# A new mixer pass: two query buffers, sums scaled first, rows before weights on ScalarE, and unread products on TensorE

## Chip, cores and metric

The kernel runs on one core of a Trainium2 chip. The core has five engines that run side by side and wait for each other through semaphores: TensorE (PE in the rows; PEld is its weight load), VectorE (DVE), ScalarE (ACT), GpSimd (POOL) and SyncE (SP, which here issues transfers). The metric is the time of one execution on the device in microseconds (us), the median of several runs.

## What is computed

The reference is one layer of a graph network over 6250 nodes with 256 features and 106250 edges.

```
xn = layernorm(x)
graph = relu([xn, mean of edge_attr per source node, u] @ W1 + b1) @ W2 + b2
m = xn
for i in range(4):                       # the mixer, four passes
    h = layernorm(m) * ln1_g[i] + ln1_b[i]
    q = softmax(h @ Wq[i], within each of 8 heads)
    k = softmax(h @ Wk[i], over the 6250 nodes)
    v = h @ Wv[i]
    m = m + (q @ (k^T v, per head)) @ Wo[i] + bo[i]
    h = layernorm(m) * ln2_g[i] + ln2_b[i]
    m = m + gelu(h @ mW1[i] + mb1[i]) @ mW2[i] + mb2[i]      # 256 -> 1024 -> 256
y = x + graph + m
out = y + (one of 32 small networks for each node, chosen by argmax of layernorm(y) @ rw^T + rb)
```

## The kernel before

**Tiles.** The nodes are 50 tiles of 125 rows. They are worked on in 25 pairs, called groups `g` (`GROUPS` = 25, `LAST` = 24). The running sum `m` stays in on-chip memory as `res`. The weights of the 256 -> 1024 -> 256 part are each kept as a high and a low half (`w1`, `w2`, as are `h1` and `hidh`), and each product is made as three products of halves (`mm3`).

**Order of the work.** Every engine has its own program. `passes(step, drain)` runs a first round of `step(-1, g)`, then `drain(-1)`, and then for the passes l = 0 to 3 the steps t = -1 to 24, with `drain(l)` behind the first three. In step (l, t) group t goes through the wide part (`up`, `gelu`, `hidden_low`, `down`, in four parts c = 0 to 3), group t + 1 through the attention's end (`transpose_queries`, `copy_queries`, `attend`, `attention_residual`, a root on GpSimd, `attention_normalise`, `attention_transpose`, `attention_high`, `attention_low`), and group t - 1 through the keys and queries of pass l + 1. The order on each engine is written out by hand, and each engine works strictly through its own list.

**The drain and the mixer's matrix.** The sums over all nodes (`acc` and `esacc`) are complete only when the last group has gone through. `drain` ends with `context`: `acc` is divided by `esacc` (two `tensor_scalar`, semaphore `c_scaled`), transposed on TensorE, made into `gn`, multiplied by Wv (`raw_vo[:, 0]`), masked into `ct`, multiplied by Wo and added to the bias: this is `mmat` (semaphore `c_ready`). `attend(l, g)` multiplies the queries of a group by `mmat`.

**Queries.** The finished softmax `qn` of a group (`softmax_queries`, `exp_queries`, `finish_queries`) is stored in device memory by SP (`store_queries`), and loaded in the next pass into the one buffer `qin` (`load_queries`, 250 KB). TensorE transposes it (`transpose_queries`, semaphore `q_T`), ScalarE copies it to `qT`. The load of group g waits until group g - 1 was transposed. In `step`, SP issues the load of group t + 2; in `drain` it issues that of group 0, after the store of the last group but one.

**Weights.** In the drain SP loads W2 into `raw` (`load_down`), after `w1` was made of the former contents of `raw`. At t = -1 ScalarE casts it to `w2`'s high half (`down_high`) and VectorE makes the low half (`down_low`). The first `down` of the pass waits for that, the first `up` for `h1`.

**GpSimd.** It takes the two roots of each step (`r1`, `r2`: one over the standard deviation), and between these it issues scatters of edge rows to device memory (L720), up to 12 a step in passes 0 to 2, for the segment sums of pass 3. The rows come in pieces through `load_attr` into `staging`.

**Pass 3** has no keys and queries of a later pass. In their place it sums edge rows per node (`seg_turn`, six pieces a step), with work on all five engines.

Of the kernel before, what the change touches and what calls it, by code (L numbers as in the profile page):

```python
# [5 lines left out]
F32 = mybir.dt.float32  # L6
# [10 lines left out]
P = 125  # L17
TILES = 50
D = 256
KC = D // 128  # L20
PAIR = 2
GROUPS = TILES // PAIR
# [23 lines left out]
IDLE_SCATTER = 48  # L46
IDLE_SEGMENT = 1
EH = 64
YROW = D + 4
# [49 lines left out]
def build(nc, x, src, edge_attr, u, gW1, gb1, gW2, gb2, Wq, Wk, Wv, Wo, bo, ln1_g, ln1_b, mW1, mb1, mW2, mb2,  # L99
# [9 lines left out]
    with ctx:  # L109
        def sb(name, shape, dt=F32, where=None):  # L110
            return (where or ctx).enter_context(nc.sbuf_tensor(name, shape, dt))
# [114 lines left out]
        qT = sb("qT", [128, KC, GT], F32, layers)  # L226
        qin = sb("qin", [P, PAIR, D], F32, layers)
        hid = [sb(f"hid{i}", [128, 2, GT], F32, layers) for i in range(2)]
# [10 lines left out]
        count16 = sb("count16", [128, KINDS - 1 + BOTH], BF16, layers)  # L239
        row16 = sb("row16", [BOTH, KINDS], BF16, layers)  # L240

        pos_f = stage[:, 0, :, :].rearrange("p c r -> p (c r)")[:, 0:ECOL]
# [94 lines left out]

        q_in, q_out, q_T, q_copied, a_prod, a_res = sems("q_in q_out q_T q_copied a_prod a_res")
        a_ve, a_root, a_xh, a_xT, a_hi, a_lo = sems("a_ve a_root a_xh a_xT a_hi a_lo")
# [32 lines left out]
        ATTR, SCATTERED = [attr0, attr1], [scattered0, scattered1]  # L372
        N_IN = [n_in0, n_in1]

# [133 lines left out]
        def _(sp):  # L508
# [44 lines left out]
            def load_queries(l, g):  # L553
                n = nth(l, g)
                sp.wait_ge(q_T, n)
                sp.wait_ge(q_out, 16 * (n + 1))
                sp.dma_start(qin[:, :, :], pair(query_rows[l % 2], g)).then_inc(q_in, 16)

# [43 lines left out]
            def step(l, t):  # L602
                if 0 <= l and t + 2 < GROUPS:
                    load_queries(l, t + 2)
                if l == 0 and t == -1:
                    load_attr(0)
                    load_attr(1)
                if l >= 0 and t == -1:
                    attr_after(l - 1, GROUPS)
                if l < LAYERS - 1 and t >= 2:  # L610
                    store_queries(l + 1, t - 2)
                attr_after(l, t)
                if l >= 0 and t == -1:
                    if l < LAYERS - 1:
                        load_mixer(l + 1)
                    if l < LAYERS - 1:
                        load_up(l + 1)
                if l == LAYERS - 1:
                    load_segments(t)

            def drain(l):
                store_queries(l + 1, LAST - 1)
                load_queries(l + 1, 0)
                load_down(l + 1)
                store_queries(l + 1, LAST)
# [176 lines left out]
        def _(act):  # L802
# [122 lines left out]
            def step(l, t):  # L925
# [7 lines left out]
                if t == -1:  # L933
                    copy_queries(l, 1)
                    down_high(l)
                segs = seg_turns(t) if l == LAYERS - 1 else ()
# [25 lines left out]
                if t + 1 < GROUPS:  # L962
                    attention_high(l, t + 1)

            def drain(l):
# [122 lines left out]
        def _(dve):  # L1088
# [353 lines left out]

            def context(l):
# [5 lines left out]
                a.then_inc(c_scaled, 1)  # L1449
                dve.wait_ge(c_T, l + 1)  # L1450
                for k in range(KC):
# [140 lines left out]
            def drain(l):  # L1592
# [20 lines left out]
                key_sum(L, final + 1)  # L1613
                add_block(L, BLOCKS - 1)
                softmax_queries(L, LAST)
                context(L)
# [182 lines left out]
        def _(pe):  # L1799
# [36 lines left out]
            def transpose_queries(l, g):  # L1836
                n = nth(l, g)
                pe.wait_ge(q_in, 16 * (n + 1))
# [4 lines left out]
                transposes(chunks(PQT), qin, P).then_inc(q_T, 1)  # L1843

# [75 lines left out]
            def queries_of(l, g):  # L1920
                m = nth(l, g)
                if l:
                    pe.wait_ge(a_res, nth(l - 1, min(g + 2, LAST)) + 1)
                if m:
                    pe.wait_ge(s_sub, m)
                for j in range(PAIR):
                    for k in range(KC):
                        a = mm(PMQ[0:P, j * D:(j + 1) * D], h2[:, k, j * P:(j + 1) * P], wqk[:, k, D:2 * D], k == 0, k == KC - 1)
                a.then_inc(s_prod, 1)

            def max_transpose(l, b):
# [103 lines left out]
            def step(l, t):  # L2035
# [21 lines left out]
                if t == -1:  # L2057
                    transpose_queries(l, 1)
                for n in segs[2:3]:
                    seg_turn(n)  # L2060
# [24 lines left out]
                if attention:  # L2085
                    attention_transpose(l, t + 1)
                if later:
                    for g in WEIGH_AT.get(t, ()):
                        weigh(l + 1, g)
# [187 lines left out]
```

## Time and profile before

| | before |
|---|---|
| median of 3 runs | 3057.9 us (3054.7 to 3060.46) |
| the profiled execution | 3049.58 us |
| its span | 3047.8 us |
| mean granted TensorE clock | 0.947 |
| TensorE busy | 2687.7 us, 88% |
| VectorE busy | 2127.8 us, 70% |
| GpSimd busy | 1724.1 us, 57% |
| ScalarE busy | 1517.9 us, 50% |

The profile is of one execution. Its own time is 8.3 us under the median of the runs shown, so differences are worked out within it and then taken from the median. The busy share is a mean over stages: which engine sets the pace of a stage is read from the waits of that stage. In the rows "[2.23 <-DVE acc L1448]" says that the engine was idle for 2.23 us before the instruction and what ended that. The clock is a share of 2.4 GHz. The passes start (first product of `up`) at about 348, 888, 1441 and 1998 us.

### The profile page before, as it was taken

What the parts mean: (1) busy time and instruction counts of PE and PEld (TensorE: products, weight loads), DVE (VectorE), ACT (ScalarE), POOL (GpSimd) and SP (SyncE); (2) the same over time, 40 slices, a digit from 0 to 9 for tenths busy, and PEclk for the clock granted to TensorE, in tenths of its full rate; (3) what the DMA queues carried; (4) which work ended last, traced back from release to release, by engine and by line L of the source; (5) the groups of instructions that cost most, each with busy time, mean ns of one, the idle gap of its engine ahead of it and who ended that gap; (6) DMA issues with size and microseconds to landing.
All of it is one profiled execution on the core that took longest, in us unless ns stands there. A gap on an engine that the chain in (4) does not pass through costs nothing.

```text
span 3047.8 us, 56121 instructions
## 1 busy us (share of the span) xinstructions
PE 2687.7 (88%) x18842; PEld 2467.5 (81%) x18842; DVE 2127.8 (70%) x4836; ACT 1517.9 (50%) x2947; POOL 1724.1 (57%) x1611
## 2 busy tenths in 40 slices
PE   4888899999989999997999999978888888996298
PEld 2666799999978899996889999868888887996165
DVE  8887567776756667675566766678888886897054
ACT  0343366566535565663556666444444444773064
POOL 0011178777758888886788887045444554222666
PEclk8999899999979999997999999889999998998599
DMA  3000223322232232323232322043333332210343
GB/s 120 24 28 24 83 50 69 66 63 58 57 97 60 63 68 62 69 53 98 58 67 61 70 60 56 26 120 90 86 83 86 83 85 58 64 43 20 82 125 92
DMA packets 255489, 207.88 MB, mean 68 GB/s; under 512 B 165433, under 2 KB 194314, under 8 KB 255205
## 3 DMA queue, kind: packets, MB, share of 16 engines
q1 hardware_dynamic: 197606, 162.55, 19.9%
q0 software_dynamic: 57600, 41.75, 6.9%
q8 instruction: 155, 2.54, 0.4%
q14 instruction: 128, 1.05, 0.1%
HBM read 136.93 MB, written 70.16 MB: 68 GB/s over the span
## 4 chain that ended last, share of the span: by engine, by line
PE 20%; POOL 14%; issue 8%; DVE 7%; ACT 2%; DMA 1%; DVEq 1%; SPq 0%; ACTq 0%; POOLq 0%; another core or an unknown queue 0%
PE bank L376 18%; POOL edges_sorted L720 9%; POOL tokens_sorted L785 2%; DVE xh L1261 2%; PE bank L1803 1%; DVE hidh_lo L1297 1%; POOL r L698 1%; PE bank L2248 1%; DVE oh L1489 1%; POOL ehl L737 1%; DVE bn L1252 1%; ACT hidh_hi L832 1%; ACT ehl L908 1%; ACT hid L826 0%; DVE res L1269 0%
## 5 line engine op out<-in xcount | busy, mean ns | idle before, releaser
L720 POOL DMA_INDIRECT edges_sorted<-staging,pos_i x850 | 1061.6, 1249 | 252.2 <-issue 231.3
L826 ACT ACTIVATE hid<-bank,b1p 128x250 f32<-128x250 f32 x800 | 331.4, 466 | 400.0 <-PE bank L376 359.0
L376 PE MATMUL bank<-h_hi,w_hi 128*128 128x250 f32 x1600 | 483.1, 302 | 19.6 <-DVE h_lo L1281 19.5
L1297 DVE TENSOR_TENSOR hidh_lo<-hid,hidh_hi 128x500 fp32r<-128x500 f32 x400 | 296.6, 742 | 290.4 <-ACT hidh_hi L832 217.0
L376 PE MATMUL bank<-w_hi,hidh_hi 128*125 128x256 f32 x1600 | 467.8, 292 | 0.0
L376 PE MATMUL bank<-h_hi,w_lo 128*128 128x250 f32 x1600 | 451.8, 282 | 0.0
L376 PE MATMUL bank<-w_hi,hidh_lo 128*125 128x256 f32 x1600 | 451.1, 282 | 0.0
L376 PE MATMUL bank<-w_lo,hidh_hi 128*125 128x256 f32 x1600 | 450.0, 281 | 0.0
L376 PE MATMUL bank<-h_lo,w_hi 128*128 128x250 f32 x1600 | 448.4, 280 | 0.0
L376 PE MATMUL bank<-wqk,h 128*125 128x256 f32 x1600 | 377.5, 390 | 0.6 <-ACT mbc L877 0.6
L376 PEld LDWEIGHTS bank<-wqk,h 128*125 128x125 f32 x1600 | 304.0, 194 | 46.2 <-issue 1.2
L376 PEld LDWEIGHTS bank<-h_hi,w_hi 128*128 128x128 f32 x1600 | 307.5, 192 | 27.5 <-DVE h_lo L1281 24.1
L832 ACT CAST hidh_hi<-hid 128x500 fp32r<-128x500 f32 x400 | 243.7, 609 | 152.2 <-PE bank L376 115.2
L376 PEld LDWEIGHTS bank<-h_lo,w_hi 128*128 128x128 f32 x1600 | 308.9, 193 | 1.9
L376 PEld LDWEIGHTS bank<-h_hi,w_lo 128*128 128x128 f32 x1600 | 305.5, 191 | 0.0
L376 PEld LDWEIGHTS bank<-w_hi,hidh_hi 128*125 128x125 f32 x1600 | 298.8, 187 | 2.0
L376 PEld LDWEIGHTS bank<-w_lo,hidh_hi 128*125 128x125 f32 x1600 | 298.0, 186 | 2.1
L376 PEld LDWEIGHTS bank<-w_hi,hidh_lo 128*125 128x125 f32 x1600 | 297.4, 186 | 0.0
L698 POOL TENSOR_TENSOR r<-ve,minus_half 125x2 f32<-125x2 f32 x175 | 136.3, 779 | 280.9 <-DVE ve L1257 277.9
L1489 DVE TENSOR_TENSOR oh<-iota_node,kb 128x1000 fp32r<-128x1000 f32 x153 | 228.7, 1495 | 59.8 <-POOL kb L732 59.7
L1261 DVE TENSOR_SCALAR xh<-res,mv,r 125x256 f32<-125x256 f32 x350 | 160.1, 498 | 135.5 <-POOL r L698 135.5
L376 PE MATMUL bank<-ehl,oh 128*125 128x130 f32 x1224 | 164.3, 278 | 65.0 <-DVE agg L1477 65.0
(289 smaller groups left out, 5712.4 us busy)
## 6 DMA issues: line engine op xcount, KB each, us to landing
staging<-edges_sorted SPq DMA_DIRECT2D x103, 260.0 KB
staging<-in_edge_attr SPq DMA_DIRECT2D x50, 531.2 KB
queries<-qn SPq DMA_DIRECT2D x100, 250.0 KB
qin<-queries SPq DMA_DIRECT2D x100, 250.0 KB
edges_sorted<-staging,pos_i POOLq DMA_INDIRECT x850
rows_in<-edges_sorted SPq DMA_DIRECT2D x50, 260.0 KB
yin<-tokens_sorted SPq DMA_DIRECT2D x81, 127.0 KB
raw<-in_L_mix_W SPq DMA_DIRECT2D x8, 1024.0 KB, 6.6
```

What stands on the lines that cost most here:

```text
L376: return nc.tensor.matmul(o, left, right, start=start, stop=stop, skip_group_check=True)
L698: nc.gpsimd.tensor_tensor(o[:, :], ve[:, :], minus_half[:, :], ALU.pow).then_inc(done, 1)
L720: nc.gpsimd.indirect_dma_start(out=edges_sorted, out_offset=bass.IndirectOffsetOnAxis(ap=pos_i[:, i:i + 1], axis=0), in_=stage[:, slot, j, ...
L737: nc.gpsimd.tensor_tensor(ehl[n % 4][:, :, EA + 2:2 * EA + 2], rows_in[n % RIN][:, :, 0:EA], f32(ehl[n % 4][:, :, 0:EA]), ALU.subtract).th ...
L785: nc.gpsimd.indirect_dma_start(out=tokens_sorted, out_offset=bass.IndirectOffsetOnAxis(ap=fpos_i[:, t:t + 1], axis=0), in_=res[:, t, :], i ...
L826: a = nc.scalar.activation(hid[c % 2][:, j, :], chunks(PH[c % 2])[:, j, :], ACT.Gelu, bias=b1p[:, 2 * c + j:2 * c + j + 1])
L832: nc.scalar.copy(hidh[c % 2][0][:, :, :], hid[c % 2][:, :, :]).then_inc(f_hi, 1)
L908: nc.scalar.copy(ehl[n % 4][:, :, 0:EA], rows_in[n % RIN][:, :, 0:EA]).then_inc(s_hi, 1)
L1252: step_(nc.vector.bn_stats(st[:, j, :], res_row(PAIR * g + j)))
L1261: a = nc.vector.tensor_scalar(o[:, j, :], res_row(PAIR * g + j), mv[:, j, 0:1], r[:, j:j + 1], ALU.subtract, ALU.mult)
L1297: nc.vector.tensor_tensor(hidh[c % 2][1][:, :, :], hid[c % 2][:, :, :], f32(hidh[c % 2][0][:, :, :]), ALU.subtract).then_inc(f_lo, 1)
L1489: nc.vector.tensor_tensor(oh[n % 4][:, :, :], iota_node[:, :].unsqueeze(1).to_broadcast((128, SEGR, P)), kb[:, n % 4, :].unsqueeze(2).to_b ...
```

## The change

- There are two buffers `qin0`, `qin1` with a semaphore each. Group g + 2 may be loaded once group g was transposed. In `step` SP issues the load of group t + 3. In `drain` it issues those of groups 0 and 1, ahead of the last two stores.
- On VectorE the division of `acc` is a function of its own, `context_scale`, and runs ahead of `softmax_queries` of the last group.
- On ScalarE, at t = -1, `down_high` runs after `attention_high`, and a two-element Gelu (`warm_gelu`) between them.
- On TensorE, at t = -1, eight products of 128 columns whose result nobody reads follow the transposes of group 1's queries, and five more follow the transposes of group 0's `xh1`. They go to bank `PS`.

```
+IDLE_RESIDUAL, IDLE_HALVES = 8, 5
...
             def load_queries(l, g):
                 n = nth(l, g)
-                sp.wait_ge(q_T, n)
+                if n >= 2:
+                    sp.wait_ge(q_T, n - 1)
                 sp.wait_ge(q_out, 16 * (n + 1))
-                sp.dma_start(qin[:, :, :], pair(query_rows[l % 2], g)).then_inc(q_in, 16)
+                sp.dma_start(qin[n % 2][:, :, :], pair(query_rows[l % 2], g)).then_inc(Q_IN[n % 2], 16)
...
             def step(l, t):                                    # SP
-                if 0 <= l and t + 2 < GROUPS:
-                    load_queries(l, t + 2)
+                if 0 <= l and t + 3 < GROUPS:
+                    load_queries(l, t + 3)
...
             def drain(l):                                      # SP
+                load_queries(l + 1, 0)
+                load_queries(l + 1, 1)
                 store_queries(l + 1, LAST - 1)
-                load_queries(l + 1, 0)
                 load_down(l + 1)
                 store_queries(l + 1, LAST)
...
                 if t == -1:                                    # ScalarE, step
                     copy_queries(l, 1)
-                    down_high(l)
...
                 if t + 1 < GROUPS:
                     attention_high(l, t + 1)
+                if t == -1:
+                    warm_gelu()
+                    down_high(l)
...
-            def context(l):                                    # VectorE
+            def context_scale(l):
                 dve.wait_ge(g_acc, block(l, BLOCKS - 1) + 1)
                 step_(nc.vector.reciprocal(esrec[:, :], esacc[:, :]))
                 stepped()
                 for k in range(KC):
                     a = nc.vector.tensor_scalar(acc[:, k, :], acc[:, k, :], esrec[:, k:k + 1], None, ALU.mult)
                 a.then_inc(c_scaled, 1)
+
+            def context(l):
                 dve.wait_ge(c_T, l + 1)
...
                 add_block(L, BLOCKS - 1)                       # VectorE, drain
+                context_scale(L)
                 softmax_queries(L, LAST)
                 context(L)
...
             def transpose_queries(l, g):                       # TensorE
                 n = nth(l, g)
-                pe.wait_ge(q_in, 16 * (n + 1))
+                pe.wait_ge(Q_IN[n % 2], 16 * (n // 2 + 1))
...
-                transposes(chunks(PQT), qin, P).then_inc(q_T, 1)
+                transposes(chunks(PQT), qin[n % 2], P).then_inc(q_T, 1)
...
+            def idle_products(count):
+
+                for _ in range(count):
+                    mm(PS[:, 0:128], ident[:, :], ones[:, :], True, True)
...
                 if t == -1:                                    # TensorE, step
                     transpose_queries(l, 1)
+                    idle_products(IDLE_RESIDUAL)
...
                 if attention:
                     attention_transpose(l, t + 1)
+                if t == -1:
+                    idle_products(IDLE_HALVES)
```

## Rows read from the trace of the kernel before

**Rows 1.** Waits, whole run: engine, line waited for: us in total, times, longest.

```profile
PE bank L1803 <- DMA qin<-queries: 26.0, 5, 7.2
```

**Rows 2.** Timeline of TensorE, start of pass 1: start us, us, instructions.

```profile
865.65 0.66 PE L1982 MATMUL bank<-ident,acc 128*128 128x128 f32 x4 [2.23 <-DVE acc L1448]
...
867.39 2.08 PE L376 MATMUL bank<-gn,raw_vo 128*128 128x128 f32 x8
...
872.97 3.75 PE L376 MATMUL bank<-mmat,qT 128*125 128x256 f32 x8 [0.90 <-issue]
883.01 1.10 PE L1803 MATMUL bank<-ident,qin 125*128 125x125 f32 x4 [6.29 <-DMA qin<-queries]
883.90 1.04 PE L1803 MATMUL bank<-ident,xh 125*128 125x125 f32 x4
887.76 0.58 PE L376 MATMUL bank<-h_hi,w_hi 128*128 128x250 f32 x1 [2.82 <-DVE h_lo L1281]
```

**Rows 3.** Timeline of VectorE, end of the drain and start of pass 1.

```profile
861.93 0.87 DVE L1392 SCALAR_TENSOR_TENSOR acc<-acc,fexp_k,bank 128x256 f32<-128x256 f32 x2
863.45 0.69 DVE L1402 TENSOR_REDUCE qstat<-bank 125x16 f32<-125x512 f32 x1 [0.65 <-PE bank L376]
...
864.78 0.15 DVE L1445 RECIPROCAL esrec<-esacc 128x2 f32<-128x2 f32 x1
...
866.34 0.99 DVE L1452 TENSOR_SCALAR gn<-bank,cols 128x256 f32<-128x256 f32 x2 [0.75 <-PE bank L1982]
...
879.56 0.73 DVE L1261 TENSOR_SCALAR xh<-res,mv,r 125x256 f32<-125x256 f32 x2 [0.84 <-POOL r L698]
...
888.22 2.28 DVE L1440 TENSOR_TENSOR w_lo<-raw,w_hi 128x2048 fp32r<-128x2048 f32 x1
```

**Rows 4.** Timeline of ScalarE, start of pass 1.

```profile
884.62 1.90 ACT L896 CAST w_hi<-raw 128x2048 fp32r<-128x2048 f32 x1
886.41 0.58 ACT L846 CAST h_hi<-bank 128x500 fp32r<-128x500 f32 x1
890.75 1.28 ACT L826 ACT_TABLE_LOAD   x1 [3.76 <-issue]
```

**Rows 5.** Windows: us, each engine's busy us, granted clock, DMA share, GB/s.

```profile
866.00:873.00 7.00, 6.10 (x28) 5.10 (x26) 4.70 (x8) 1.10 (x2) 0.00 (x0) 0.54 0.04 8
873.00:877.00 4.00, 3.72 (x8) 2.45 (x8) 1.65 (x4) 0.00 (x0) 0.00 (x0) 0.52 0.83 290
877.00:880.00 3.00, 0.00 (x0) 0.00 (x0) 2.05 (x8) 0.00 (x0) 0.97 (x2) 1.00 0.31 78
...
888.00:894.00 6.00, 6.00 (x27) 5.81 (x28) 2.95 (x3) 3.21 (x6) 1.20 (x1) 0.51 0.91 257
894.00:897.00 3.00, 3.00 (x23) 2.83 (x22) 2.25 (x5) 1.05 (x3) 0.00 (x0) 1.00 0.81 302
```

**Rows 6.** Waits from 905 to 1412 us, the rest of pass 1.

```profile
DVE xh L1261 <- POOL r L698: 61.3, 29, 4.8
...
POOL r L698 <- DVE ve L1257: 0.5, 1, 0.5
```

**Rows 7.** Timeline of GpSimd, start of pass 1.

```profile
891.43 1.20 POOL L720 DMA_INDIRECT edges_sorted<-staging,pos_i  x1 [4.17 <-DMA staging<-in_edge_attr]
897.55 0.72 POOL L698 TENSOR_TENSOR r<-ve,minus_half 125x2 f32<-125x2 f32 x1 [4.92 <-DVE ve L1257]
```

**Rows 8.** Timelines of VectorE and TensorE, start of pass 3.

```profile
1989.41 5.88 DVE L1261 TENSOR_SCALAR xh<-res,mv,r 125x256 f32<-125x256 f32 x2 [0.80 <-POOL r L698]
...
1995.36 1.10 PE L1803 MATMUL bank<-ident,xh 125*128 125x125 f32 x4 [4.01 <-DVE xh L1261]
1997.83 0.58 PE L376 MATMUL bank<-h_hi,w_hi 128*128 128x250 f32 x1 [1.38 <-DVE h_lo L1281]
```

**Rows 9.** The chain in order of time, pass 3: start us, us, what.

```profile
2040.00 1.71 DVE xh L1261 x2
...
2062.29 1.71 DVE xh L1261 x2
```

More of the change, by code:

```diff
@@ L47 @@
 IDLE_SEGMENT = 1
+IDLE_RESIDUAL, IDLE_HALVES = 8, 5
 EH = 64
@@ L226, in build @@
         qT = sb("qT", [128, KC, GT], F32, layers)
-        qin = sb("qin", [P, PAIR, D], F32, layers)
+        qin0 = sb("qin0", [P, PAIR, D], F32, layers)
         hid = [sb(f"hid{i}", [128, 2, GT], F32, layers) for i in range(2)]
@@ L240, in build @@
         row16 = sb("row16", [BOTH, KINDS], BF16, layers)
+        qin1 = sb("qin1", [P, PAIR, D], F32, layers)
+        qin = [qin0, qin1]
         pos_f = stage[:, 0, :, :].rearrange("p c r -> p (c r)")[:, 0:ECOL]
@@ L335, in build @@
         w1_hi, w1_lo, w2_hi, w2_lo, b1_pe, b1_ready, b2_added = sems("w1_hi w1_lo w2_hi w2_lo b1_pe b1_ready b2_added")
-        q_in, q_out, q_T, q_copied, a_prod, a_res = sems("q_in q_out q_T q_copied a_prod a_res")
+        q_in0, q_in1, q_out, q_T, q_copied, a_prod, a_res = sems("q_in0 q_in1 q_out q_T q_copied a_prod a_res")
         a_ve, a_root, a_xh, a_xT, a_hi, a_lo = sems("a_ve a_root a_xh a_xT a_hi a_lo")
@@ L554, in load_queries @@
                 n = nth(l, g)
-                sp.wait_ge(q_T, n)
+                if n >= 2:
+                    sp.wait_ge(q_T, n - 1)
                 sp.wait_ge(q_out, 16 * (n + 1))
-                sp.dma_start(qin[:, :, :], pair(query_rows[l % 2], g)).then_inc(q_in, 16)
+                sp.dma_start(qin[n % 2][:, :, :], pair(query_rows[l % 2], g)).then_inc(Q_IN[n % 2], 16)
             def load_attr(c):
@@ L602, in step @@
             def step(l, t):
-                if 0 <= l and t + 2 < GROUPS:
-                    load_queries(l, t + 2)
+                if 0 <= l and t + 3 < GROUPS:
+                    load_queries(l, t + 3)
                 if l == 0 and t == -1:
@@ L621, in drain @@
             def drain(l):
+                load_queries(l + 1, 0)
+                load_queries(l + 1, 1)
                 store_queries(l + 1, LAST - 1)
-                load_queries(l + 1, 0)
                 load_down(l + 1)
@@ L934, in step @@
                     copy_queries(l, 1)
-                    down_high(l)
                 segs = seg_turns(t) if l == LAYERS - 1 else ()
@@ L963, in step @@
                     attention_high(l, t + 1)
+                if t == -1:
+                    warm_gelu()
+                    down_high(l)
             def drain(l):
@@ L1441, in down_low, with context_scale @@
                                         ALU.subtract).then_inc(w2_lo, 1)
-            def context(l):
+            def context_scale(l):
                 dve.wait_ge(g_acc, block(l, BLOCKS - 1) + 1)
@@ L1449, in context @@
                 a.then_inc(c_scaled, 1)
+            def context(l):
                 dve.wait_ge(c_T, l + 1)
@@ L1614, in drain @@
                 add_block(L, BLOCKS - 1)
+                context_scale(L)
                 softmax_queries(L, LAST)
@@ L1837, in transpose_queries @@
                 n = nth(l, g)
-                pe.wait_ge(q_in, 16 * (n + 1))
+                pe.wait_ge(Q_IN[n % 2], 16 * (n // 2 + 1))
                 if n:
@@ L1842, in transpose_queries @@
                 pe.wait_ge(g_acc, ALL_BLOCKS if l == LAYERS - 1 else block(l + 1, sum(s < g - 1 for s in SUM_AT)))
-                transposes(chunks(PQT), qin, P).then_inc(q_T, 1)
+                transposes(chunks(PQT), qin[n % 2], P).then_inc(q_T, 1)
             def attend(l, g):
@@ L1929, in queries_of, with idle_products @@
                 a.then_inc(s_prod, 1)
+            def idle_products(count):
+                for _ in range(count):
+                    mm(PS[:, 0:128], ident[:, :], ones[:, :], True, True)
             def max_transpose(l, b):
@@ L2058, in step @@
                     transpose_queries(l, 1)
+                    idle_products(IDLE_RESIDUAL)
                 for n in segs[2:3]:
@@ L2086, in step @@
                     attention_transpose(l, t + 1)
+                if t == -1:
+                    idle_products(IDLE_HALVES)
                 if later:
```

2 lines of the change are left out of this document (1 added, 1 removed).

## The prediction

> **What bounds the kernel now.** I read the waits first. One of them is special: five times TensorE waits for a transfer into `qin`, 26.0 us together, 7.2 us the longest [rows 1]. Four of these are the four mixer passes' starts, the fifth is 0.3 us. So I went on to the start of the second pass; the passes are numbered 0 to 3 here, and the other starts have the same form.
>
> The timeline of TensorE there reads as follows [rows 2]. The transposes of `acc` at 865.65 come after 2.23 us of standing still for VectorE. The mixer's matrix `mmat` is then built. At 872.97 the eight products of `attend` begin. The next thing in TensorE's order is the transpose of the second query pair, and it starts only at 883.01, when its transfer has landed. SP issues that transfer only behind the drain's last store. The transposes of `xh1` are behind it. The first product of `up` comes at 887.76. On VectorE `xh1` was finished at 879.56 + 0.73 = 880.29 [rows 3], so it stood ready for 3.6 us. On ScalarE the cast of all of `w2` (1.90 us from 884.62) runs ahead of the cast of `h1` at 886.41 [rows 4], although the transposes of `xh1` ended at 883.90 + 1.04 = 884.94 [rows 2]. TensorE is at half its clock (0.51 to 0.54, which is 1.2 GHz) from 866 to 873 and again from 888 to 894, and back at 1.00 only from 894 [rows 5].
>
> Does time won at a pass's start reach the end? It does if the engine that paces the pass is moved too. In the first pass that is TensorE. In the second it is GpSimd: VectorE waits 29 times for GpSimd's roots, 61.3 us, while GpSimd waits for VectorE's variances once, 0.5 us [rows 6]. Its scatters stand in one queue with those roots. So what counts in passes 1 and 2 is when GpSimd takes the second root of the pass (897.55, after an idle time of 4.92 us for VectorE) [rows 7].
>
> **The change, part by part.**
>
> *Sums scaled first* (`context_scale` ahead of `softmax_queries`). Now the last `acc` operation ends at 861.93 + 0.87 = 862.80. VectorE waits until 863.45 for the product of queries and does the softmax, and only then, from 864.78, scales `acc` [rows 3]. TensorE follows at 865.65 [rows 2] and `gn` at 866.34. Afterwards the scaling (865.65 - 864.78 = 0.87 us with its reciprocal and the signal) starts at 862.8 and is done about 863.7, the transposes run 863.7 to 864.4, and the softmax (1.33 us from start to start) runs beside them and ends near 865.0. So `gn` starts at 865.0 instead of 866.34: **1.3 us**, in four passes. What waits on the softmax is `exp_queries` on ScalarE, behind a copy of `qT` that comes much later; it costs nothing.
>
> *Two buffers and earlier loads.* In the drain both first loads are issued ahead of the last two stores. Both conditions (the row stored, the buffer's earlier pair transposed) were met some steps before, so SP's queue isn't held there, and both transfers (250 KB) have some 20 us. In `step` each load goes one pair further. Its wait on `q_T` is still for the same transpose as before, so what is queued behind it on SP (attributes, stores, mixer weights) is not held longer. The load of pair 2 takes the place of that of pair 1 in SP's queue, with the same bytes. The transposes of pair 1 then follow `attend` at once, and the wait for `qin` is gone.
>
> *Rows ahead of weights on ScalarE.* `attention_high` comes before `down_high`. How long the way from `xh1` to `up` is without both obstacles is shown by pass 3, where `xh1` itself is late: from its end (1989.41 + 5.88 = 1995.29) to the transposes 0.07 us, and from these (1995.36) to the first product of `up` (1997.83) 2.47 us [rows 8]. So `up` would start 2.54 us after `xh1`: at 880.29 + 2.54 = 882.83 instead of 887.76, **4.9 us** in pass 1. The same three rows of passes 0 and 2 give 4.6 and 4.7 us. In pass 3 neither obstacle ends last, so **0**.
>
> What is late instead is `w2`. After `h1`'s cast come the table load (1.28 us at 890.75 now [rows 4]), a two-element Gelu (I take 0.2 us) and the 1.90 us cast. In pass 1, without the 1.3 us: transposes of `xh1` 880.4 to 881.5, `h1`'s cast to 882.1, table 883.4, Gelu 883.6, `w2_hi` 885.5, and with VectorE's 2.28 us [rows 3] `w2_lo` 887.8. The first product of `down` comes behind two parts of `up`, `attend` and a third part after 882.8: at the low clock 24 x 0.22 + 2 + 1.4 us, so 891.5, at the full clock about 888.7. The cover is 3.7 or 0.9 us; beyond it each us would count. The table load leaves the way of the first Gelu. The Trainium skill, ScalarE: Activation LUTs, "What ACT_TABLE_LOAD costs", adds a drain of 1.38 us to the load. The trace has no row that shows it here; with it `w2_lo` would be at 889.2, still covered at the low clock, and the sum would stay.
>
> *Unread products.* Eight of 128 columns between pair 1's transposes and those of `xh1`, and five behind these. The nearest row is `gn`'s: eight of 128x128 in 2.08 us at the low clock [rows 2]. `attend` ends at 876.7, the transposes at 877.6, eight products at 879.5; `xh1` is ready at 880.3. Five take 1.3 us of the 1.4 us in which ScalarE and VectorE make `h1`. Cost 0, at worst 0.3 us a pass. What they give depends on the clock. The dense `attend` (3.72 us busy of 4) is followed by a clock of 1.00 after 877, which is wasted now because TensorE then stands still. The 27 products of 888 to 894 take 0.22 us each and the 23 of 894 to 897 0.13 [rows 5], so 24 products of `up` at full clock save 2.2 us, `attend` up to 1.8 more. From below the products change nothing (0), from above all of that is saved in passes 0 to 2. I take about half of the 2.2 in pass 0, 1.0 us. In pass 2 I take 0.5, because the second root also waits for `hidden_low` behind `down_low`. In pass 1 I take 0, see below. The shorter stop before `acc`'s transposes might keep the clock up through the context too. That would be worth up to 3.3 us a pass (`gn`'s and `ct`'s products and `attend`), but narrow products fill that stretch, so I take 1.4 us over four passes.
>
> *Where GpSimd limits it.* In pass 1 it has issued five scatters and waits until 891.43 for attributes [rows 7]. These are issued after the same waits as before, so they land 1.3 us earlier, 890.1. One scatter of 1.2 us and its gap later, at 891.5, it can take the second root. VectorE has that variance at about 897.5 - 6.2 = 891.3. So pass 1 gains 6.0 us and nothing more from the clock. Pass 2 has no such wait.
>
> *Pass 3.* The 1.3 us are partly lost: `down_low` (2.28 us) now waits for the later cast on ScalarE (`h1`'s to 1995.8, then 1.28 + 0.2 + 1.90 us, so 1999.2) and its low half about 2001.5. The two selections of edge rows behind that on VectorE start hardly sooner than now. I take 0.5 us.
>
> **Sum.** Pass 0: 1.3 + 4.6 + 1.0 = 6.9. Pass 1: 6.0. Pass 2: 1.3 + 4.7 + 0.5 = 6.5. Pass 3: 0.5. Context clock: 1.4. Together 21.3 us. The profiled execution took 3049.6 us (span 3047.8), so it would be 3028.3. The median of the runs shown is 3057.9, 8.3 us above it, and against that the forecast is **3036 us**. Less than 0.2%, some 6 us, can't be told from no change.
>
> **The rivals.**
>
> *The clock holds* (0.16). With the gaps filled, TensorE stays at 2.4 GHz from the context through `up`: 3.3 us x 4 for the context, 2.9 for pass 0 and 1.5 for pass 2 in place of 1.4 + 1.0 + 0.5, so 14.7 more: 36 us, 3022. For it: the clock is granted after `attend` in all four passes. Against it: after the eight products 0.8 us stay empty, and more at the high clock. The Trainium skill, TensorE: Matmul & The Clock Gate, "What's actually happening", says that throttled is the default and that sustained activity releases it; by that rule it would come out so, and the clock of 1.00 right after `attend` agrees, that of 0.54 through a busy context doesn't.
>
> *GpSimd and its attributes keep the pace* (0.12). If pair 2's transfer and the attributes land no earlier, say 5 us later than I count, the second root of passes 1 and 2 comes where it did, and their 4.9 and 4.7 us are gone: 21.3 - 9.6 = 12 us, 3046. For it is the wait until 891.43, against it the equal bytes in the same order.
>
> *It moves nothing that counts* (0.05): passes 0 to 2 keep their step by something that I haven't seen: 3052 to 3064.
>
> *Slower* (0.05). Pass 3 has a locked step, 2040.00 to 2062.29, so 22.29 us [rows 9]. ScalarE's first casts of edge rows now come behind `w2`, and GpSimd, VectorE and TensorE meet them in another phase. If they lock into a step that is longer by more than 21.3 / 24 = 0.9 us, the gain is used up, and at 1.2 us it ends at 3036 + 29 = 3065. For it: three engines are near their limit there. Against it: the step is the same to 0.01 us for most of the pass, which looks like a cycle that any start would fall into.
>
> **How the numbers follow.** Forecast 0.62, own range 3029 to 3043: the sum with clock terms at 0 is 18.4 us (3039.5), and a gain of pass 3 of 0 or a late product takes 2 more. The range for 8 in 10 takes in most of both neighbours: 3024 to 3049. Faster by over 0.2%: 0.62 + 0.16 + 0.12 = 0.90. Same 0.05, slower 0.05.
>
> **What would show it.** Right: no wait of TensorE for `qin`. `gn` 1.3 us closer to the last `acc`. From `xh1`'s end to `up` 2.5 us in passes 0 to 2. The table load ahead of `w2`'s cast. The second root of pass 1 right behind a scatter. Steps afterwards as long as now. Wrong: `xh1`'s transposes behind the unread products; the first `down` waiting for `w2_lo`; attributes of pass 1 landing after 16 us of their issue; another step in pass 3 than 22.29 us. If the clock reads 1.00 over the context, the gain is nearer 36 us.

## The result, and the profile after

The changed kernel takes 3026.0 us (median of 6 runs, 3019.5 to 3029.9) beside 3059.2 us for the kernel before in the same session (6 runs, 3053.4 to 3064.3). The ratio is 0.9891, with a 95% interval of 0.9876 to 0.9906: faster by 33.2 us, where 21.3 us were forecast. The two profiled executions have spans of 3024.2 and 3047.8 us.

All times that follow are counted from the end of the last `acc` operation of a drain, so that passes and kernels can be laid side by side. They are read from the timelines, "before > after".

| | pass 0 | pass 1 | pass 2 | pass 3 |
|---|---|---|---|---|
| `gn` starts | 3.54 > 2.09 | 3.54 > 2.09 | 3.54 > 2.40 | 3.55 > 2.09 |
| `mmat` starts | 9.37 > 7.37 | 9.38 > 7.39 | 9.58 > 6.37 | 9.56 > 7.38 |
| `attend` takes | 3.75 > 1.96 | 3.75 > 1.96 | 3.59 > 1.96 | 3.61 > 1.96 |
| `xh1` is done | 17.56 > 13.78 | 17.49 > 13.72 | 17.53 > 12.70 | 26.23 > 24.27 |
| first `up` | 24.73 > 15.86 | 24.96 > 15.81 | 24.76 > 14.78 | 28.77 > 27.22 |
| first `down` | 32.20 > 21.91 | 33.80 > 21.84 | 33.52 > 20.83 | 38.11 > 37.80 |
| second root | 34.53 > 23.86 | 34.75 > 27.74 | 34.56 > 22.79 | 41.58 > 41.29 |
| next `acc` | 539.54 > 528.65 | 553.33 > 548.30 | 552.93 > 537.28 | |

Pass 3, up to its last addition into `agg`, took 595.8 and 595.6 us. So the passes give 10.9, 5.0, 15.7 and 0.2 us. The last stage is another matter: from the first load of `yin` to the end 162.1 us passed before and 169.1 us after, and no edit touches that stage. That is why the spans differ by 23.6 us although that load starts 30.6 us earlier. (31.8 us are won in the passes, of which 1.3 are lost again because the first `acc` came that much later in this execution.)

TensorE at the start of pass 1, kernel after (timeline, as [rows 2]):

```profile
854.14 0.66 PE L1998 MATMUL bank<-ident,acc 128*128 128x128 f32 x4 [0.29 <-DVE acc L1456]
...
856.37 1.63 PE L380 MATMUL bank<-gn,raw_vo 128*128 128x128 f32 x8 [0.79 <-DVE gn L1462]
...
861.42 1.96 PE L380 MATMUL bank<-mmat,qT 128*125 128x256 f32 x8 [0.91 <-issue]
863.22 0.59 PE L1814 MATMUL bank<-ident,qin 125*128 125x125 f32 x4
863.65 1.95 PE L380 MATMUL bank<-ones,ident 128*128 128x128 f32 x16
867.02 0.65 PE L1814 MATMUL bank<-ident,xh 125*128 125x125 f32 x4 [1.42 <-DVE xh L1269]
867.50 1.28 PE L380 MATMUL bank<-ones,ident 128*128 128x128 f32 x10
869.05 0.38 PE L380 MATMUL bank<-h_hi,w_hi 128*128 128x250 f32 x1 [0.26 <-issue]
```

The wait for `qin` is gone, and the stop ahead of `acc`'s transposes fell from 2.23 to 0.29 us. `attend` takes 1.96 instead of 3.75 us. The unread products ("ones,ident"; each stands as two records) end 1.42 us ahead of the transposes of `xh1` and 0.26 us ahead of `up`, so they delay neither. The two transposes behind `attend` take 0.59 and 0.65 us instead of 1.10 and 1.04.

ScalarE and VectorE behind `xh1` in pass 1, kernel after (timelines, as [rows 3, 4]):

```profile
867.70 0.57 ACT L852 CAST h_hi<-bank 128x500 fp32r<-128x500 f32 x1 [3.28 <-PE bank L1814]
868.30 1.28 ACT L905 ACT_TABLE_LOAD   x1
869.59 0.20 ACT L905 ACTIVATE gelu_warm<-gelu_warm 1x1 f32<-1x1 f32 x1
869.70 1.88 ACT L902 CAST w_hi<-raw 128x2048 fp32r<-128x2048 f32 x1
...
871.62 2.29 DVE L1448 TENSOR_TENSOR w_lo<-raw,w_hi 128x2048 fp32r<-128x2048 f32 x1 [2.03 <-ACT w_hi L902]
```

`w_lo` is ready at 873.91. The first `down` starts at 875.08, so 1.2 us of cover are left.

TensorE's clock in pass 1, kernel after (windows, columns as in [rows 5]):

```profile
853.00:856.00 3.00, 2.30 (x16) 1.75 (x15) 2.90 (x8) 0.00 (x0) 1.59 (x2) 1.00 0.16 29
856.00:859.00 3.00, 2.63 (x13) 2.56 (x14) 2.54 (x5) 0.12 (x1) 0.00 (x0) 0.65 0.00 0
...
861.00:863.00 2.00, 1.58 (x7) 1.42 (x8) 1.86 (x4) 0.00 (x0) 0.00 (x0) 1.00 0.78 267
863.00:866.00 3.00, 2.60 (x22) 2.33 (x20) 1.86 (x6) 0.57 (x1) 0.53 (x1) 1.00 0.68 236
869.00:875.00 6.00, 5.95 (x44) 5.73 (x45) 3.97 (x4) 5.24 (x9) 5.08 (x5) 1.00 0.45 110
```

Before, the windows showed the low level (1.2 GHz) from 866 to 877 and again from 880 (0.52 up to 888) to 894, where 27 products ran in the last 6 us [rows 5]. Now it is low for some 3 us of the context only. It is at 2.4 GHz in `attend`, and 44 products of `up` run in 6 us.

GpSimd and SP's queue at the start of pass 1, kernel after (timelines, as [rows 7]):

```profile
872.51 2.44 POOL L726 DMA_INDIRECT edges_sorted<-staging,pos_i  x1 [0.30 <-issue]
874.96 0.23 POOL L723 COPY staging<-src_f 125x17 f32<-125x17 f32 x1
879.76 1.19 POOL L726 DMA_INDIRECT edges_sorted<-staging,pos_i  x1 [4.57 <-DMA staging<-in_edge_attr]
880.98 0.74 POOL L704 TENSOR_TENSOR r<-ve,minus_half 125x2 f32<-125x2 f32 x1
```

```profile
863.70 0.46 SPq L568 DMA_DIRECT2D staging<-in_edge_attr  x1
864.25 11.82 SPq L530 DMA_DIRECT2D wqk<-in_L_mix_Wk  x1
876.11 0.46 SPq L531 DMA_DIRECT2D wqk<-in_L_mix_Wq  x1
```

The second root no longer waits for VectorE; it stands right behind a scatter, and that scatter waited 4.57 us for edge attributes that landed 16.1 us after their issue. In the rest of the pass the waits have the old form (as [rows 6], window from 884 to 1398 us, 7 us longer than the one before):

```profile
DVE xh L1269 <- POOL r L704: 71.7, 33, 4.2
```

The start of pass 3, kernel after, VectorE and GpSimd (timelines, as [rows 8]):

```profile
1953.99 0.42 DVE L1300 TENSOR_TENSOR b_b<-b_b,gb_b 125x256 f32<-125x256 f32 x1 [5.49 <-DMA gb_b<-in_L_gnn_b]
...
1957.21 5.88 DVE L1269 TENSOR_SCALAR xh<-res,mv,r 125x256 f32<-125x256 f32 x2 [0.80 <-POOL r L704]
```

```profile
1957.12 5.51 POOL L734 MEMSET agg<- 125x6500 f32 x1
```

VectorE waits 5.49 us for the graph's bias, and then `xh1` takes 5.88 us beside a memset of 5.51 us on GpSimd; elsewhere the same operation takes 0.73 us. Behind it `w2`'s low half and the two selections of edge rows (`oh`) run back to back on VectorE, and TensorE waits for the first selection ahead of its first `down`:

```profile
1968.20 2.29 DVE L1448 TENSOR_TENSOR w_lo<-raw,w_hi 128x2048 fp32r<-128x2048 f32 x1 [2.03 <-ACT w_hi L902]
...
1970.63 4.23 DVE L1499 TENSOR_TENSOR oh<-iota_node,kb 128x1000 fp32r<-128x1000 f32 x2
```

```profile
1972.70 1.59 PE L380 MATMUL bank<-ehl,oh 128*125 128x130 f32 x8 [1.79 <-DVE oh L1499]
```

The locked step behind is as it was (as [rows 9]; chain in order of time):

```profile
2009.50 1.71 DVE xh L1269 x2
2031.78 1.71 DVE xh L1269 x2
```

### The profile page after: what moved, and what is told of

Same layout as the page of the kernel before. It is cut to its first block, busy times and chain, and to the rows that moved or that the text cites. A ratio compares the mean times of both kernels' runs of the same rounds, so it can differ in the third digit from the quotient of the medians.

```text
span 3024.2 us, 56331 instructions
## 1 busy us (share of the span) xinstructions
PE 2684.0 (89%) x18946; PEld 2464.8 (82%) x18946; DVE 2130.8 (70%) x4836; ACT 1517.7 (50%) x2951; POOL 1725.8 (57%) x1611
## 3 DMA queue, kind: packets, MB, share of 16 engines
q8 instruction: 155, 2.54, 0.4%
## 4 chain that ended last, share of the span: by engine, by line
PE 39%; POOL 28%; issue 13%; DVE 13%; DMA 3%; ACT 2%; DVEq 1%; SPq 0%; ACTq 0%; another core or an unknown queue 0%; POOLq 0%
PE bank L380 35%; POOL edges_sorted L726 22%; PE bank L1814 3%; POOL r L704 3%; POOL tokens_sorted L791 2%; DMA staging<-in_edge_attr 2%; DVE xh L1269 2%; DVE hidh_lo L1305 1%; PE bank L2267 1%; POOL ehl L743 1%; DVE oh L1499 1%; DVE bn L1260 1%; DVE staging L1178 1%; DVE kmask L1172 1%; DVE res L1277 1%
```

## The experiments

Each group was run beside the kernel before on one chip. The chips differ (its median was 3050.4, 3030.1 and 3032.7 us), so kernels are compared within a group, or by their ratios. The unedited changed kernel was run in the first and the third group; in the second, kernels are set against its ratios (0.9887 to 0.9898) and its profile of the first group. A ratio comes with its 95% interval; it isn't the plain quotient of the two medians given, and can differ from it by 0.001 (3 us). "Root 2" is GpSimd's second root of a pass. All kernels compute the whole reference; the unread products don't enter it.

### First group: the edits one at a time (before: 3050.4 us)

**The changed kernel again**, unedited.

> The changed kernel again, beside the three that undo one part each, so that all four share the runs of the kernel before. Ratio to the kernel before 0.989 +- 0.002. If the profiled execution of the kernel before was 8 us under its median by chance, the ratio of the medians stays near 0.989 and not near the 0.992 that the two profiled spans give.

3013.7 us, ratio 0.9887 [0.9867, 0.9907]. As expected. Root 2 at 23.72, 27.80 and 22.81 us: the starts of passes 0 to 2 in the table above repeat to 0.2 us.

**No unread products.**

```
-IDLE_RESIDUAL, IDLE_HALVES = 8, 5
+IDLE_RESIDUAL, IDLE_HALVES = 0, 0
```

> Both counts of unread products are 0, all else as changed. Theory A (they hold the full clock from attend to up): TensorE is at half clock again in the first products of up, passes 0 and 2 lose 3 to 4 us each, pass 1 at most 1 because GpSimd's second root waits for attributes, so 5 to 9 us over the changed kernel, ratio to before 0.991 to 0.992. Rival B (the clock holds because the waits are gone, the products do nothing): within 2 us of the changed kernel, 0.989.

3020.9 us, 0.9911 [0.9889, 0.9933], 7.2 us above the changed kernel, as theory A had it, though the two intervals overlap. TensorE, pass 1 (timeline and windows):

```profile
862.55 1.96 PE L380 MATMUL bank<-mmat,qT 128*125 128x256 f32 x8 [0.90 <-issue]
864.35 0.59 PE L1814 MATMUL bank<-ident,qin 125*128 125x125 f32 x4
868.15 1.10 PE L1814 MATMUL bank<-ident,xh 125*128 125x125 f32 x4 [3.21 <-DVE xh L1269]
870.62 0.58 PE L380 MATMUL bank<-h_hi,w_hi 128*128 128x250 f32 x1 [1.38 <-DVE h_lo L1289]
```

```profile
870.00:876.00 6.00, 5.38 (x27) 5.32 (x28) 3.98 (x4) 4.88 (x7) 5.09 (x4) 0.58 0.44 110
876.00:879.00 3.00, 3.00 (x23) 2.83 (x22) 1.83 (x5) 1.32 (x4) 0.75 (x2) 1.00 0.64 126
```

`attend` still runs at full clock. After a stop of 3.21 us the clock is back at its low level and stays there through the first products of `up`, as before the change. `up` starts only 0.5 us later, but the first `down` 2.4, 2.4 and 2.0 us. This is what the unread products buy. The Trainium skill, TensorE: Matmul & The Clock Gate, "What's actually happening", has sustained activity release the throttle; the pair of 0.58 without them and 1.00 with them agrees. Up to root 2 the three passes lose only 2.4 us together; 6.8 us more lie behind it. Passes 0 and 2 lose 1.6 and 1.3 us there, not the 3 to 4 of theory A; pass 1 loses nothing. Two executions of the kernel before differ behind root 2 by 5.8 us too (below), so between 2 and 9 us is what these runs allow. What the eight and the five products do singly was not run.

**Sums scaled late again.**

```
-                context_scale(L)
                 softmax_queries(L, LAST)
+                context_scale(L)
```

> The sums are scaled after the last queries' softmax again, all else as changed. If that part is worth only its place on the chain: 1.4 us in each of passes 0 to 2, some of it in pass 3, so 4 to 5.5 us over the changed kernel (0.9905). If the stop of 2.2 us also costs the clock in the context: 8 to 12 us over it (0.992 to 0.993), and pass 2 shows half clock between the transposes of acc and attend, where the changed kernel's profile shows the full one.

3030.5 us, 0.9935 [0.9911, 0.9959], 16.8 us above the changed kernel. TensorE's stop ahead of `acc`'s transposes is 2.23 us again (timeline):

```profile
855.40 0.67 PE L1998 MATMUL bank<-ident,acc 128*128 128x128 f32 x4 [2.23 <-DVE acc L1456]
```

`gn` starts at 3.55 us. `mmat` starts at 9.63, 9.65, 8.76 and 9.62 us, so 2.2 to 2.4 us later, and in two of four passes `attend` takes 3.54 us. Root 2 comes 4.0, 2.2 and 2.4 us later. These 8.6 us are the edit's. The two profiles differ by 22.0 us; of the rest, 4.6 us lie behind the roots of passes 0 to 2, 1.7 in pass 3 and 4.9 in the last stage, and I can't assign them. At the roots scaling first is worth more than its 1.45 us on the chain, because the clock comes back sooner. The half clock that the expectation named for pass 2 is there (`mmat` 2.4 us later), while `attend` behind it is at the full one.

**Weights first again.**

```
                     copy_queries(l, 1)
+                    down_high(l)
...
-                if t == -1:
-                    warm_gelu()
-                    down_high(l)
```

> On ScalarE the cast of w2 runs ahead of that of h1 again, and the early Gelu is left out, all else as changed. By the chain: the 1.9 us cast stands before h1 only if W2 has landed by then; then up is 1.5 to 2 us later in passes 0 and 2, less in pass 1 where attributes cap it, 0 in pass 3: 3 to 5 us over the changed kernel (0.990 to 0.991). If W2 lands later than the transposes of xh1, more: up to 3 us a pass, 9 us (0.992). The table load comes back in front of the first Gelu and costs nothing by itself.

3017.1 us, 0.9894 [0.9874, 0.9915]: 3.4 us above the changed kernel by the medians, as expected, but the intervals of this and the unedited kernel nearly coincide. The first `up` starts at 15.87, 15.80 and 15.04 us, the first `down` at 21.89, 21.84 and 21.07: the same to 0.3 us. With the queries there, TensorE is done with pair 1's transposes before `xh1` is ready, and the cast of `w2` fits into ScalarE's wait, but barely: it begins when W2 has landed and ends 0.25 us ahead of the cast of `h1` in pass 1 (ScalarE, timeline), and in pass 2 it holds that cast.

```profile
862.34 1.90 ACT L902 CAST w_hi<-raw 128x2048 fp32r<-128x2048 f32 x1 [1.13 <-DMA raw<-in_L_mix_W]
864.49 0.57 ACT L852 CAST h_hi<-bank 128x500 fp32r<-128x500 f32 x1 [0.25 <-PE bank L1812]
```

Root 2 comes at 24.40, 27.90 and 23.58 us, so 0.7, 0.1 and 0.8 us later: with the table load in front of the first Gelu again, that Gelu starts 0.6 us later in pass 1. Pass 3 goes the other way. The low half of `w2` is ready 2.0 us sooner and the pass takes 593.2 instead of 595.6 us; some 1 us of that was already won at `xh1`, in a context that kept the clock. So the new order is worth 1.6 us at three roots and may cost about as much in pass 3; in the total nothing shows beyond the intervals. What it would do without the second buffer was not run.

### Second group: buffers, and what limits the passes (before: 3030.1 us)

**One buffer, all else as changed.**

```
-        qin = [qin0, qin1]
+        qin = [qin0, qin0]
...
-                if n >= 2:
-                    sp.wait_ge(q_T, n - 1)
+                sp.wait_ge(q_T, n)
```

with the loads where they were in the kernel before.

> One buffer and the old order of the loads again, all else as changed. Theory A (the wait for the transfer was the main part): the transposes of the second query pair wait for it again, the eight unread products and the transposes of xh1 follow; up comes some 23 us after the last acc operation instead of 15.8 in passes 0 and 2, the second root of pass 1 some 5 us later, pass 3 unchanged: 18 to 22 us over the changed kernel, ratio 0.994 to 0.996. Rival (the clock and the context made most of the gain): 8 us or less over it, 0.991.

3023.4 us, 0.9981 [0.9972, 0.9991]. By the ratios that is some 27 us over the changed kernel, more than the 18 to 22 of theory A, and the rival (8 us or less) falls. The first `up` starts at 23.60, 24.00 and 23.71 us, root 2 of pass 1 is 4.2 us later. TensorE waits 35.8 us for `qin`, more than before [rows 1], since it gets there earlier. Pass 1 (timeline):

```profile
870.36 1.96 PE L380 MATMUL bank<-mmat,qT 128*125 128x256 f32 x8 [0.90 <-issue]
881.04 1.10 PE L1812 MATMUL bank<-ident,qin 125*128 125x125 f32 x4 [8.71 <-DMA qin<-queries]
```

So scaling first, the new order and the unread products are worth 6.6 us without the second buffer (5.8 by the ratio). Most of what they win in front of the transfer is waited away at it. The run undoes the buffer and the earlier place of the loads together; neither was run alone.

**Attributes of the next pass ahead of `load_down` in SP's queue.**

```
                 store_queries(l + 1, LAST - 1)
+                attr_after(l, GROUPS)
...
-                if l >= 0 and t == -1:
-                    attr_after(l - 1, GROUPS)
```

> SP issues the drain's loads of edge attributes ahead of the loads of W2 instead of behind the last store, all else as changed. If the second root of pass 1 waits for these attributes alone: it comes 23.7 us after the last acc operation instead of 27.8, and pass 1 is 3 to 4 us shorter (545 to 541 us from acc to acc), ratio 0.987 to 0.988. If GpSimd's own scatters pace the pass anyway: the root is earlier and the pass gets 1 us or nothing.

2996.9 us, 0.9894 [0.9879, 0.9908]. GpSimd, pass 1 (timeline):

```profile
871.67 1.20 POOL L725 DMA_INDIRECT edges_sorted<-staging,pos_i  x1 [0.30 <-POOL staging L722]
873.22 0.72 POOL L703 TENSOR_TENSOR r<-ve,minus_half 125x2 f32<-125x2 f32 x1 [0.36 <-DVE ve L1264]
```

The wait for attributes is gone; root 2 of pass 1 comes at 23.80 instead of 27.80 us, as in pass 0. Of these 4.0 us, 3.1 reach the end of the pass (541.80 for 544.89 in the first group). The attributes were what held root 2 of pass 1. At the end of the pass that is 0.1% of the whole, less than the ratio's interval, and the ratio itself is not under the changed kernel's; 0.987 to 0.988 had been expected.

**Six unread products in the context**, behind the bias of `up`.

```
                 up_bias(l, range(6, FC))
+                idle_products(6)
```

> Six more unread products in the context, behind the narrow products and before those of gn, all else as changed. If the stop and the narrow products cost the clock there: full clock from acc to attend in all passes, mmat 6.4 us after the last acc operation in each (7.4 in passes 0, 1 and 3 of the changed kernel), 2 to 3 us less in all (0.988). If the clock falls anyway: the six take 1.4 us in a gap of 0.8, and each pass is 0.5 us longer (0.990).

3000.7 us, 0.9908 [0.9894, 0.9922]. The clock reads 1.00 through all four contexts, and `mmat` starts at 6.45, 6.45, 6.77 and 6.46 us. In the changed kernel that is 7.24, 7.38, 6.38 and 7.40, so passes 0 and 1 win 0.8 and 0.9 us and pass 2, whose clock held without help, loses 0.4. From `acc` to `acc` 524.89, 545.00 and 537.12 beside 526.17, 544.89 and 537.07: at most 1.3 us. The clock did as the first theory says, the 2 to 3 us did not come: the ratio is no better than the changed kernel's.

**The graph's bias later in pass 3**: VectorE's `graph_bias` moved behind `attention_low`.

```
                     attention_low(l, t + 1)
+                    if l == LAYERS - 1 and t == -1:
+                        graph_bias()
```

> In pass 3 the sum of the two output biases is taken behind attention_low instead of ahead of the first residual, so VectorE does not wait there for a transfer, and xh1 is made before GpSimd's long memset; all else as changed. Theory A (that wait is why pass 3 gained nothing): xh1 ends 13.7 us after the last acc operation instead of 24.3, and the pass is 5 to 9 us shorter, ratio 0.986 to 0.987. Rival (the edge rows set the pace there, which wait for the last store of queries): up is early, but the first down is not, and the gain is 0 to 2 us.

2994.5 us, 0.9888 [0.9874, 0.9903]. VectorE in pass 3 (timeline):

```profile
1938.85 0.73 DVE L1269 TENSOR_SCALAR xh<-res,mv,r 125x256 f32<-125x256 f32 x2 [0.81 <-POOL r L704]
1940.93 0.68 DVE L1289 TENSOR_TENSOR h_lo<-bank,h_hi 128x500 fp32r<-128x500 f32 x1 [1.35 <-ACT h_hi L852]
1941.86 0.42 DVE L1300 TENSOR_TENSOR b_b<-b_b,gb_b 125x256 f32<-125x256 f32 x1 [0.25 <-DMA gb_b<-in_L_gnn_b]
...
1944.24 2.29 DVE L1448 TENSOR_TENSOR w_lo<-raw,w_hi 128x2048 fp32r<-128x2048 f32 x1 [1.24 <-ACT w_hi L902]
```

GpSimd beside it:

```profile
1944.42 5.51 POOL L734 MEMSET agg<- 125x6500 f32 x1 [5.61 <-DMA queries<-qn]
```

`xh1` is done at 12.35 us instead of 24.3, and takes 0.73 us, since GpSimd's memset now comes at 1944.42. Pass 3 takes 586.9 instead of 595.6 us. What the new pass start won and pass 3 did not show was hidden behind this wait and this collision; the edit removes both at once, so their shares stay open. The rival has its part too: the first `down` begins at 29.5 us, 15.1 us behind `up`, because the memset waits for the last store of queries and the selections of edge rows for the memset. The 8.7 us are in the profile; the ratio over all executions is within the changed kernel's, above the 0.986 to 0.987 expected, and the profiled execution was the fastest of four.

### Third group: scatter, the buffers alone, all together (before: 3032.7 us)

**The kernel before again**, unedited.

> The kernel before against itself, for a second profile of it and for what the comparison makes of no change: ratio 1.000 +- 0.002. The starts of the passes read as in its first profile to 0.3 us. If the 3.9 us that pass 2 gained behind its start are the change's, this pass takes 518 us again from the second root to the last acc operation; if they are chance, it takes less.

0.9997 [0.9987, 1.0006]. From root 2 to the next `acc` 501.8, 517.9 and 516.5 us, in the first profile 505.0, 518.6 and 518.4. In pass 3 `attend` took 1.96 us this time, and root 2 came 1.2 us sooner; the other starts repeat to 0.4 us. Pass 2 took 516.5 us from root 2, between the two answers.

**The changed kernel a third time.**

> The changed kernel beside the two others of this call, on the same chip: ratio 0.989 to 0.990.

3002.3 us, 0.9898 [0.9883, 0.9913]. The clock held through the context of pass 1 (`mmat` at 6.05 us), and in pass 3 `attend` took 3.75 us.

**Two buffers alone**: all other edits undone (the diffs of the first group together).

> The two buffers and the earlier loads alone: sums scaled late, w2's cast ahead of h1's, no unread products. If the buffers carry the gain: up 20.1 us after the last acc operation instead of 24.8 in passes 0 to 2, with w2's cast finished before xh1, so 14 to 16 us faster than before, ratio 0.995; the rest of the change then gives as much again through the clock and the context. If w2's cast still stands in the way: up at 21.5 to 22, 9 to 11 us, 0.997.

3013.9 us, 0.9929 [0.9916, 0.9943], 18.8 us under the kernel before (21.5 by the ratio), where 14 to 16 were expected. The first `up` starts at 18.29, 17.64 and 20.01 us, the first `down` at 26.74, 25.43 and 27.94. Root 2 comes 6.4, 5.6 and 4.7 us sooner than in the kernel before beside it. TensorE stops for 3.1 to 3.3 us ahead of `xh1`'s transposes and has the low clock in `up`, as without the unread products. In three of the four passes `attend` takes 1.96 us although TensorE had stopped for 2.23 us ahead of `acc`'s transposes.

**Attributes early, unread products in the context, and the bias late, together**, on top of the change.

> The changed kernel with the attributes' loads early, six unread products in the context and the bias sum of pass 3 late. The sum of what the three gave alone in the profiles: 3 us in pass 1, 1 us in passes 0 and 2 together, and now 1 in pass 1, where the attributes no longer cap it; 8.7 us in pass 3, of which the stage behind kept 2.5. Together 10 to 14 us under the changed kernel, ratio 0.985 to 0.986. If they don't add: 0.987.

2984.2 us, 0.9844 [0.9831, 0.9858]: 18.1 us under the changed kernel beside it, more than the 10 to 14 expected, and the fastest version here. Pass 1, GpSimd (timeline), and TensorE's clock (windows):

```profile
871.85 0.72 POOL L703 TENSOR_TENSOR r<-ve,minus_half 125x2 f32<-125x2 f32 x1 [0.36 <-DVE ve L1264]
```

```profile
852.00:855.00 3.00, 2.91 (x23) 2.54 (x22) 2.62 (x5) 0.86 (x2) 0.00 (x0) 1.00 0.00 0
...
863.00:869.00 6.00, 5.74 (x43) 5.33 (x42) 3.86 (x4) 5.91 (x10) 5.09 (x4) 1.00 0.62 182
```

Root 2 comes at 22.93, 22.86 and 22.87 us. Against the changed kernel beside it the passes take 1.8, 4.9, 1.9 and 8.6 us less, and the first `acc` is done 0.9 us earlier.

## Why the prediction was right, and where it was short

The direction held, and so did the mechanism of the waits; the size was short by 12 us, because the clock's share was priced far too low. The measured 3026 us lies inside the wide range, below the forecast's own range (3029 to 3043), and nearer to the rival "the clock holds" (3022) than to the forecast (3036; 3057.9 less 21.3 is 3036.6). The profile lays the gain up to root 2 out like this:

| us earlier | pass 0 | pass 1 | pass 2 |
|---|---|---|---|
| `gn` | 1.45 | 1.45 | 1.14 |
| `gn` to `mmat` | 0.55 | 0.54 | 2.07 |
| `mmat` to `xh1` done | 1.78 | 1.78 | 1.62 |
| `xh1` to `up` | 5.09 | 5.38 | 5.15 |
| `up` to `down` | 1.42 | 2.81 | 2.71 |
| `down` to root 2 | 0.38 | -4.95 | -0.92 |
| sum | 10.67 | 7.01 | 11.77 |

**Sums scaled first: right, and too small.** 1.3 us were forecast and 1.45 measured (1.14 in pass 2). Its second effect, the shorter stop, I had named and priced too low (see the clock).

**The wait for `qin`: right.** The one-buffer kernel brings it back (35.8 us), the buffers alone give more than half of the gain. Whether the parts add up is less clear. Without the second buffer the rest is worth 8.8 us at the three roots, behind it 12.3. By the medians it is 6.6 and 11.6 us (30.4 less 18.8 in the third group), by the ratios 5.8 and 9.4, and their intervals, some 3 to 6 us each way, overlap.

**Rows ahead of weights: wrong.** `xh1` to `up` took 2.08 to 2.09 us where I forecast 2.54, the rest being the clock. But the forecast takes both obstacles away for their whole length, which gives some 1.4 us a pass to the new order on ScalarE (`h1`'s cast at 886.41, the transposes done at 884.94), and with the old order `up` is at most 0.3 us later and root 2 at most 0.8. Two obstacles stood on one way, the transfer and the cast; I read them from a trace in which both were late, and did not ask whether the second remains once the first is gone. Its cast then ends within 0.4 us of the transposes of `xh1`, ahead of them in passes 0 and 1.

**TensorE's clock: the term that was mis-sized.** The forecast gave it 1.0 us in pass 0, 0.5 in pass 2, nothing in pass 1 and 1.4 for all contexts, 2.9 together. Measured, the rows "`gn` to `mmat`", "`mmat` to `xh1` done" and "`up` to `down`" hold 3.75, 5.13 and 6.40 us in passes 0, 1 and 2; with 0.44 us between the transposes of `xh1` and `up` (2.47 to 2.03) that is some 16.6 us in three passes. The stretch from `gn` to `xh1` has 8.3 of them, the products of `up` the other 8.3 (the table load that moved has no part in it: with weights first, `down` comes as soon), and without the unread products `down` comes 6.8 us later in the three passes together. Pass 1's share was capped by the attributes. Passes 0 and 2 kept some 10 us, where 1.5 and part of the 1.4 had been forecast. Two steps failed. I held that the narrow products of the context would keep the clock down up to and through `attend`, and took half of the product term for caution. It does fall there, but for some 3 us in place of some 10, and is back ahead of `attend`. Over all profiles, `attend` ran at full clock in 6 of 16 passes where TensorE had stopped 2.23 us ahead of `acc`'s transposes, and in 39 of 40 where it had stopped 0.29 to 0.68 us. The stop doesn't decide alone: of the 16, the kernel before has 1 of 8, the two kernels with a second buffer 5 of 8, and why is open. The eight and five products then carry the clock to `up`. What I had as a rival with 0.16 was half true (its 2.9 us for pass 0 has no row behind it; the products of `up` were put at 2.2): the context itself still falls to the low level in most passes (0.65 above), the rest of passes 0 to 2 does not. Holding it there as well is worth next to nothing (at most 1.3 us).

**Pass 1 capped by attributes: right.** Forecast: attributes at 890.1 and root 2 at 891.5, so 27.3 and 28.7 us behind `acc`. Measured: 26.5 and 27.7. It gained 7.0 us at root 2 for 6.0 forecast, and 5.0 at the end of the pass. With the attributes early, root 2 came 4.0 us sooner: that they held it is shown.

**Pass 2** gained 11.8 us at root 2 and 3.9 behind it. The second execution of the kernel before shows that 1.8 of the 3.9 can be chance; the remaining 2 stay open.

**Pass 3: the number right, the reason only in part.** It gained 0.2 us for 0.5, and the step is still 22.28 to 22.30 us, so the slower rival fell. I had named the late `w2` and the selections of edge rows behind it, and that is on the way: `oh` starts right behind `w2`'s low half, TensorE waits 1.79 us for it, and the two selections take 4.23 us beside GpSimd's work on `ehl`, for 2.31 us in the kernel before and in the one with weights first, where GpSimd is idle then. What I left out stands in front of it. `xh1` itself is late by the wait for the bias and by the memset, 24.3 us for 13.7 in pass 1, and with the bias late the pass is 8.7 us shorter. That the sum came out is luck in that respect.

The Trainium skill, Trainium Architecture — The Big Picture, "What this means for kernel authors", calls the port that VectorE and GpSimd share an exclusive lock. The 5.88 us beside the memset and 0.73 without it agree. It doesn't hit every operation: with the bias late, `w2`'s low half runs beside the same memset and takes 2.29 us, as without it; nor is the memset longer (5.51 us).

**Late `w2`: right.** It was ready 1.2 us ahead of `down`; at the full clock I had 0.9. That holds for passes 0 to 2, and for `down` itself; for pass 3 see above. The early Gelu is of one element, not of two. The drain of 1.38 us that the Trainium skill, ScalarE: Activation LUTs, "What ACT_TABLE_LOAD costs", adds to a table load does not show here: `h_hi` ends at 868.27, the load runs from 868.30, the Gelu starts at 869.59. With that drain `down` would have waited 0.2 us.

**The rest of the miss.** The passes gave 31.8 us in the two profiles, and the medians differ by 33.2; the last stage varied by 7 us the other way and the first `acc` by 1.3, which is why the spans differ by 23.6 only. So it was right to work the gain out within one execution and to take it from the median.

## What to carry to other kernels

When two waits end at the same place, cost each with the other taken away: the second obstacle here all but vanished with the first, and of four edits one shows nothing in the total. A stall on TensorE can cost more than its own length, because the products behind it may run at half speed; price the stretch behind a stop at both levels, and look in more than one execution which of them it gets. What is won ahead of the next late thing (a transfer, attributes, a bias) is lost there, so look for it in each pass by itself.

## What the runs showed that I had not expected

- The same two kernels differ by about 1% between the four occasions (before: 3059, 3050, 3030 and 3033 us), while the ratio after to before stays within 0.9887 to 0.9898. Most of it lies in the last stage: 162 to 169 us in the profiles of the first result and the first group, 147 to 150 in the second and third.
- Whether TensorE's clock falls in the context differs between executions of one kernel: pass 1 of the changed kernel had `mmat` at 7.39, 7.38 and 6.05 us.
- The issue of the transfer of `wqk` behind the attributes held SP's queue for 11.82 us in pass 1; with the attributes ahead of it in the drain it took 0.41 us.
